# Layer 2 of a graph network on Trainium2: the fetches of edge scores wait for the last but one, on two semaphores

## The reference

```
z  = einsum('ni,hif->nhf', h, W)           # h: layer norm of x
el = einsum('nhf,hf->nh', z, a_l);  er = einsum('nhf,hf->nh', z, a_r)
e  = leaky_relu(el[src] + er[dst], 0.2)
m  = segment_max(e, dst);  ex = exp(e - m[dst]);  s = segment_sum(ex, dst)
out = segment_sum((ex / s[dst])[:, :, None] * z[src], dst)
```

## Time and profile before

| | us |
|---|---|
| Median of 3 runs | 3426.36 |
| Lowest and highest | 3422.85, 3426.89 |
| The profiled execution | 3417.09 |
| Its span on the core | 3415.1 |
| PE busy in the span | 2743.4 (80%) |
| DVE busy | 2437.6 (71%) |
| ACT busy | 1672.9 (49%) |
| POOL busy | 1665.0 (49%) |

### The profile page before, as it was taken

How to read it: one execution, slowest core, us unless ns; L and a number is a source line. 1 busy time by engine, 2 the same in 40 slices (tenths; PEclk the granted TensorE clock), 3 DMA queues, 4 the chain that set the end, 5 groups by cost and what they waited for, 6 DMA issues and landing times. The chain is left out here.

```text
span 3415.1 us, 49827 instructions
## 1 busy us (share of the span) xinstructions
PE 2743.4 (80%) x13389; PEld 2146.2 (63%) x13389; DVE 2437.6 (71%) x5315; ACT 1672.9 (49%) x3377; POOL 1665.0 (49%) x1473
## 2 busy tenths in 40 slices
PE   4999699999979962111179998999999969689997
PEld 3888544444457741010067776888888868578886
DVE  8557699999976740000068787999999988667776
ACT  3565533333345330000034434999999955356665
POOL 2788567666646547777600001555555533124433
PEclk9999899999999985555589999999999989789999
DMA  4433699999920400000000002988888865478886
GB/s 169 113 90 103 208 349 346 345 346 348 342 77 25 149 8 2 8 2 2 8 19 19 25 26 82 309 306 308 309 307 309 302 226 188 170 226 230 229 234 166
DMA packets 197471, 600.30 MB, mean 176 GB/s; under 512 B 42764, under 2 KB 52355, under 8 KB 196175
## 3 DMA queue, kind: packets, MB, share of 16 engines
q0 software_dynamic: 135040, 429.23, 39.5%
q1 hardware_dynamic: 62286, 169.29, 14.1%
HBM read 513.25 MB, written 84.95 MB: 175 GB/s over the span
## 5 line engine op out<-in xcount | busy, mean ns | idle before, releaser
L662 POOL DMA_INDIRECT g_rows<-z_rows,edge_src x704 | 721.1, 1024 | 888.8 <-POOLq L155 416.3
L1377 DVE TENSOR_REDUCE t_largest<-t_masked 128x4 f32<-128x512 f32 x352 | 234.5, 685 | 414.5 <-DMA edge_list<-payload,row_i 256.5
L1214 PE MATMUL t_masked<-t_never,t_apart 128*128 128x512 f32 x352 | 156.6, 445 | 363.4 <-issue 261.5
L1510 PE MATMUL g_sums<-g_rows,g_share 128*128 128x256 f32 x1760 | 445.9, 388 | 1.2 <-issue 0.7
L1130 POOL DMA_INDIRECT shared<-el_rows,edge_src x352 | 353.1, 1003 | 187.8 <-issue 115.2
L703 ACT ACTIVATE g_scaled_hi<-g_rows,edge_weight_sorted 128x1024 fp32r<-128x1024 f32 x176 | 202.6, 1151 | 355.5 <-DMA g_rows<-z_rows,edge_src 349.2
L717 PE MATMUL g_sums<-g_rows,g_share 128*128 128x512 f32 x704 | 333.3, 596 | 21.1 <-DMA g_rows<-z_rows,edge_src 21.1
L1510 PEld LDWEIGHTS g_sums<-g_rows,g_share 128*128 128x128 f32 x1760 | 309.0, 191 | 34.6 <-issue 1.1
L1214 PEld LDWEIGHTS t_masked<-t_never,t_apart 128*128 128x128 f32 x352 | 70.6, 201 | 405.2 <-issue 350.0
L330 POOL DMA_INDIRECT edge_list<-payload,row_i x196 | 260.8, 1330 | 126.0 <-issue 116.5
L738 DVE SCALAR_TENSOR_TENSOR g_scaled_lo<-g_rows,edge_weight_sorted,g_scaled_hi 128x1024 fp32r<-128x1024 f32 x176 | 225.5, 1281 | 48.6 <-ACT g_scaled_hi L703 31.3
(11 more groups left out here) (407 smaller groups left out, 7536.1 us busy)
## 6 DMA issues: line engine op xcount, KB each, us to landing
e_raw<-in_L_ffn_rw_dram SPq DMA_DIRECT2D x28, 1024.0 KB
g_rows<-z_rows,edge_src POOLq DMA_INDIRECT x704
g_place_of<-place_rows SPq DMA_DIRECT2D x44, 256.0 KB
z_rows<-z_zout SPq DMA_DIRECT2D x20, 512.0 KB
x_rows<-x_all SPq DMA_DIRECT2D x20, 512.0 KB
z_rows<-t_zout SPq DMA_DIRECT2D x20, 512.0 KB
s_x<-x_rows SPq DMA_DIRECT2D x20, 512.0 KB
xn_rows<-s_rows SPq DMA_DIRECT2D x10, 1024.0 KB
```

The source lines that it names most:

```text
L662: pool.indirect_dma_start(out=r.rows[:, slot, :], out_offset=None, in_=table, in_offset=bass.IndirectOffsetOnAxis(ap=g.src[:, i * GT + q:i ...
L1214: t.matmul(masked[:, n % 3, :], apart[:, n % 8, :], never[:].rearrange("p h n -> p (h n)"), start=True, stop=False)
L1377: v.tensor_reduce(largest[:, q, :], masked[:, n % 3, :].rearrange("p (h n) -> p h n", h=HEADS), AX.X, ALU.max).then_inc(taken, 1)
L1510: t.matmul(sums[:, it.buf(2), h // 2, h % 2 * HF:(h % 2 + 1) * HF], share[:, it.buf(2), n, :], r.rows[:, it.buf(4) * GT + q, h * HF:(h + 1 ...
```

## The change

POOL gets a wait ahead of each fetch: fetch n waits until fetch n - 2 has landed (the first two wait for nothing more). The 23 semaphores `el_in[b]` become two, taken in turn by even and odd chunks. DVE's wait for a batch becomes two waits, one on each semaphore, for the count that both have when all fetches of the batch have landed. Nothing that is computed changes.

```diff
+EL_RING = 2
@@ stage_attention
-        el_in = [sem(f"el_in{b}") for b in range(NB)]
+        el_in = [sem(f"el_in{k}") for k in range(EL_RING)]
@@ block.gpsimd
             for n in range(NE):
+                at_least(pool, el_in[n % EL_RING], n // EL_RING * 16)
                 q.indirect_dma_start(
                     out=g.edge_el[:, n, :], out_offset=None, in_=g.el,
                     in_offset=bass.IndirectOffsetOnAxis(ap=g.src[:, n:n + 1], axis=0),
-                ).then_inc(el_in[BATCH_OF[n]], 16)
+                ).then_inc(el_in[n % EL_RING], 16)
@@ block.vector, parts(b)
-                dve.wait_ge(el_in[b], 16 * size)
+                for k in range(EL_RING):
+                    dve.wait_ge(el_in[k], (BATCH_AT[b] + size) // EL_RING * 16)
```

## The result

The kernel after took 3409.94 us (median of 9, 3405.67 to 3419.56) beside 3422.85 for the kernel before (9 runs, 3419.86 to 3426.89): a ratio of 0.9962, 95% interval [0.9951, 0.9974]. It is 13 us faster, where 347 were forecast. The profiled execution of after is its longest (3419.56 us); its span is 3417.4 us.

A forecast was written before the change was run, and what follows sets the result against it. PE's signals, late beside POOL's unwaited fetches, were taken to bound layer 2's masks. With fetches 1.43 us apart the last reduction comes 350.7 us earlier: 3417.1 - 350.7 + 9.3, forecast 3076 us, range 3010 to 3320.

The forecast's parts named there:

- Where the time was: Layer 2's masked stage: for some 430 us, while POOL fetches, it runs ten times slower than it can.
- the 1684 that the prediction gave for compute alone: Masked stage: first mask at about 1258 us, then 352 chunks at 1.21 us end at 1684 us.
- What is late: Masked stage: PE's signal to DVE and ACT arrives some 10 us late, and the lateness comes with the fetches.
- Step (3), "what goes": Masked stage: the unwaited run of fetches goes, and PE's lateness with it; chunks then go at 1.21 us, fetches bound.
- Step (1), the spacing: POOL's 350 added waits: fetches stand 1.43 us apart, with ends of 1.26 and 2.03 us.
- The 16 us that DVE's splits might have added: DVE's batch splits lock POOL out of a shared port: up to 16 us longer; nothing was added for it.
- Step (2), two semaphores at nothing: DVE's one more wait at each of 23 batches: 0 to 5 us, taken as 0.
- The sum: Masked stage: last fetch issued at 1733.1 us, last reduction at 1761.7 instead of 2112.4; total 3076 us.
- with a spacing of 1.26 ... 1705, 3019: Fast end for the fetches: last reduction at 1705 us, 407 us less, total 3019 us.
- The lateness stays: Rival, masked stage: 16-byte gathers themselves may cause the lateness; 3426 us at unchanged spacing, 3458 at 1.43; chance 0.10.
- The wait inherits the lateness: Rival, POOL's waits: fetches' increments arrive 7 to 10 us late, spacing 4.5 us, total 4154 us; chance 0.08.
- PE's clock doesn't come back: Rival, masked stage: PE stays at 1.2 GHz, about 2.1 us a chunk, 115 us less, 3311 us; chance 0.08.

The follow-up runs named there:

- no_fetch: Kernel after without its 352 fetches of edge scores and their waits, scores zero: 2981.97 us, beside 3420.09 for the kernel before.
- after_again: The kernel after, unchanged, on a chip where the kernel before took 3005.63 us: 3064.48 us, ratio 1.0195.
- ring4: Kernel after with four semaphores in turn, each fetch waiting for the fourth last: 3009.47 us beside 3007.2 for the kernel before, ratio 1.0015.
- spaced: Kernel after, with POOL clearing a scratch of 512 columns after each fetch: 3357.27 us beside 3420.09 for the kernel before, ratio 0.9818.
- ring1: Kernel after with one semaphore, each fetch waiting until the last one landed: 3521.01 us beside 3420.09 for the kernel before, ratio 1.0297.
- wide512: Kernel after, fetching rows of 512 bytes into a scratch, scores left zero: 3097.7 us beside 3420.09 for the kernel before.

## Why the prediction was wrong

*Where the time was*: right. 430 us of the stage were a stall that comes with the fetches; taking them away gives back 438 us on the late chip (no_fetch), and its last reduction, at 1672.4 us, is near the 1684 that the prediction gave for compute alone.

*What is late* was misread, though the conclusion that PE's signals are late stands. The prediction took the reduction of 1714.40 for the answer to the product of 1703.27 ("some 10 us late") and that of 1725.65 for the answer to the product of 1724.98 ("as it ends"). By count they are the 30th and the 32nd, of masks whose products began at 1666.87 and 1703.27. The delay is 48 us for the one and still 22 us for the other: at 1725.65 the queue was being worked off, it hadn't gone.

*Step (3), "what goes", failed.* It let the lateness end with the unwaited run of fetches. It compared this stage with two others and found two differences in the code, the waits and the semaphores, and took them for the cause, while it said itself that no row told why. With 350 waits and two semaphores the fetches stand 1.39 us apart instead of 1.33, and the lateness is unchanged, 2.80 us for each PE instruction as before: 36 reductions up to 1737.6 us where the prediction wanted hundreds, and 13 us gained where 347 were forecast. So the 23 semaphores aren't the cause, nor is it enough to put a wait before each fetch. As only 80 of the waits bit, the run doesn't refute that an issue which really stands still would help. What ends the lateness on that chip is no fetch at all, or fetches 2.28 us apart or more, or rows of 512 bytes at 1.55 us. The comparison with the scatters (one per 1.66 us) and the gathers (1.51 us) was called "alike" in rate; since 1.39 is late and 1.55 with longer rows isn't, that small difference may have mattered. The runs can't say so for certain, and the cause stays open.

*Step (1), the spacing*: right in size where it can be tested, on the prompt chip: 1.46 us against 1.43 forecast. Its landing of 1.95 + 0.4 = 2.35 us after the start is the 2.4 of the landing row; the 0.4 was an estimate without a row, and lucky. The issue was 0.95 us and not 1.04. The 0.12 us by which 1.46 is over (2.4 + 0.27)/2 = 1.34 I put to landings of up to 4.3 us, whose delay is never made up; no run separates it. On the late chip the 1.39 is no test of this sum, since few of the waits bit. The 16 us that DVE's splits might have added to the fetches aren't there either: in after_again the issues average 0.954 us, against a median of 0.950, 1.4 us more in all.

*Step (2), two semaphores at nothing*: right, by ring4 to within 8 us.

*The sum* is right where the lateness is absent, and there it has nothing to win against: the last reduction was put at 1761.7 us and stands at 1760.4 in after_again, the total at 3076 and is 3064.5. That the last reduction fits to 1.3 us is luck: the last fetch was put at 1733.1 and is issued at 1743.6, and the work behind it was put at 28.6 us and took 16.8. But the kernel before ends at 3005.6 there. So the added waits alone cost 59 us on a prompt chip, and the forecast of "faster" has its sign wrong there. The prediction's own line "with a spacing of 1.26 ... 1705, 3019" is the kernel before on a prompt chip: 1704.0 and 3005.6.

*The rivals.* "The lateness stays" came true on the late chip; it had a chance of 0.10. Its price was set at 0 to 32 us longer for a slow phase that grows with the fetches. The phase did grow at its end, 1737.6 against 1727.5 us (by the start of the quick reductions), but the median fell by 13. Of the forecast's 35 us of growth only 10 came, since the first quick reduction stands 10 us behind the last fetch and not 29 (1727.5 - 1698.6). Where the 13 us come from isn't visible: the profiled executions of the two kernels are 2.3 us apart the other way (spans 3417.4 and 3415.1), so the difference of the medians has no trace. It stays open. "The wait inherits the lateness" falls: POOL's longest wait was 1.4 us in a stretch where DVE's was 25.1. (Its price of 7 to 10 us came from the miscount above.) "PE's clock doesn't come back" falls too: 0.94 in after_again's stage, with PE waiting at each batch, 0.97 in after behind the last fetch. At longer waits it does sink, to 0.78 in spaced and 0.73 in ring1 over the same stretch, where the fetches were the bound, the last reduction 19 us behind the last fetch in both:

```profile
1270.00:1700.00 430.00, 242.78 (x980) 189.05 (x980) 189.48 (x437) 91.79 (x230) 284.36 (x379) 0.78 0.07 14
```

```profile
1270.00:1700.00 430.00, 202.31 (x810) 157.46 (x810) 153.10 (x361) 75.68 (x190) 153.61 (x162) 0.73 0.06 11
```

The first is spaced, the second ring1. The Trainium skill's rule to issue a DMA early and wait on it late (page "DMA: Bandwidth & Descriptors", section "Rules for kernel authors") has the prompt chips' sign: four in flight 3009 us, two 3064, beside 3007 and 3006 for before. For one in flight only the late chip was measured.

*What stays open*: why PE's signals fall behind beside these fetches on one chip (or at one time) and on six others don't; and whether on it the pace, the length of the rows, the number in flight or POOL's standing still decides between 1.39 and 2.28 us. The page just named, section "Why a DMA increments its semaphore by 16 and not by 1", says that each engine which takes part in a DMA writes its own increment. At 16 for each fetch, fetches 1.39 us apart would be 11 or 12 such writes per us, an estimate that rests on that page. Whether these writes compete with PE's signals no run here shows; wide512, with as many increments per fetch at 1.55 us, was not late.

## What to carry to other kernels

A stall that the trace puts to "remote" or to a semaphore of an earlier stage, with all engines idle, may be the chip's and not the program's: before it is priced as a gain, time the kernel on a second chip and at another time, for one chip's trace can't tell, and 415 of 3420 us hung on it here. To say how late a signal is, count both sides: the signal that an engine waits for need not be that of the last instruction before it, and whether the gaps go by time or by the sender's instructions tells a fixed delay from a queue. A cause taken from "what differs in the code" is a guess until a run removes the suspected work altogether; no_fetch would have told in one run which work it is, and what it costs on that chip. The depth of a wait has its own price, which one can work out: with n transfers in flight the spacing is the landing time plus the answer, over n, plus the tail of late landings, and never under the pace of issuing (1.26 us here); two in flight cost 59 us here and four at most 8.

## What the runs showed of the hardware

- A chip on which, while POOL issues 16-byte gathers every 1.33 to 1.39 us, the other engines learn of PE's instructions one per 2.8 us, so that, once they have fallen behind, masks are taken 35 to 60 us after their product began; at 2.28 us between gathers they aren't late. On two others the traces of 16-byte gathers every 1.26 to 1.27 us show none of it, and on six in all the kernel before takes 3003 to 3011 us. On the late chip landings reached POOL in time meanwhile: it was never held for more than 1.4 us.
- A gather of 128 rows of 16 bytes lands 2.1 to 4.3 us after its start, median 2.4. Rows of 512 bytes cost hardly more per fetch: 1.28 us apart with four in flight, against 1.26 for 16-byte rows.
- On the late chip the fetches of after stood closer (1.39 us) than on a prompt one (1.46), with 80 waits that bit against 266. DVE, ACT and the stores mostly stood still beside them there; that this is the reason is argued, not shown.
